# Cross-attention block: one copy carries a slot of k and q together, into rows six partitions apart

## The reference, cut to what matters

```python
x = layer_norm(hidden_states, ln1_w, ln1_b)
q = (x @ q_w + q_b).reshape(B, LQ, H, HD).transpose(0, 2, 1, 3)
k = (encoder_hidden_states @ k_w + k_b).reshape(B, LK, H, HD).transpose(0, 2, 1, 3)
v = (encoder_hidden_states @ v_w + v_b).reshape(B, LK, H, HD).transpose(0, 2, 1, 3)
scores = jnp.einsum('bhqd,bhkd->bhqk', q, k) * scale
scores = jnp.where(mask, scores, mask_value)
attn = jax.nn.softmax(scores, axis=-1)
out = jnp.einsum('bhqk,bhkd->bhqd', attn, v)
out = out.transpose(0, 2, 1, 3).reshape(B, LQ, D)
hidden = out @ cproj_w + cproj_b + residual
y = layer_norm(hidden, ln2_w, ln2_b)
y = jax.nn.gelu(y @ fc_w + fc_b, approximate=True)
return hidden + y @ proj_w + proj_b
```

## Time and profile before

| | |
|---|---|
| median of 3 runs | 260.54 us |
| lowest and highest | 257.79 and 260.97 us |
| the profiled execution | 260.51 us |
| its span on the core | 258.7 us |
| mean granted clock of PE | 0.921 of full |

### The profile page before, as it was taken

The page is one execution under the profiler, slowest core; times in us unless marked ns, Lnnn a source line. Parts: engine busy times, 40 slices in busy tenths (PEclk is TensorE's granted clock), DMA queues, the critical chain, the costliest instruction groups (busy, mean ns, idle before and its releaser), DMA issues.

```text
span 258.7 us, 7970 instructions
## 1 busy us (share of the span) xinstructions
PE 216.3 (84%) x3324; PEld 200.9 (78%) x3324; DVE 173.4 (67%) x377; ACT 123.8 (48%) x269; POOL 86.9 (34%) x100
## 2 busy tenths in 40 slices
PE   0974089759979999999699995999999988699795
PEld 0974069649968988989599895989998987599695
DVE  2683046495799768977687593767896669349661
ACT  3568203128922785378305960278338813541050
POOL 5345121113842085128410751128414511212300
PEclk9998559776999999999979996799999999779999
DMA  6999992006900395049801892059406930100011
GB/s 204 292 208 225 186 160 90 4 8 114 125 7 4 109 179 86 5 136 141 98 3 50 172 127 27 5 159 151 62 4 121 130 44 3 44 0 3 3 41 41
DMA packets 24255, 23.10 MB, mean 89 GB/s; under 512 B 2908, under 2 KB 23964, under 8 KB 24220
## 3 DMA queue, kind: packets, MB, share of 16 engines
q1 hardware_dynamic: 21616, 19.75, 43.7%
q10 hardware_dynamic: 2604, 2.85, 4.5%
HBM read 7.62 MB, written 2.10 MB: 38 GB/s over the span
## 4 chain that ended last, share of the span: by engine, by line
PE 41%; DVE 19%; DMA 15%; SPq 13%; issue 8%; ACT 3%; POOL 1%; ACTq 0%; POOLq 0%; DVEq 0%
PE bank L1049 11%; SPq L341 10%; PE bank L1051 8%; PE bank L1050 8%; DMA k_stack<-part_k 8%; DMA k_stack<-mask_rows 5%; PE bank L1123 4%; DVE mx L813 4%; DVE recip L859 3%; PE scores L1079 3%; DVE g_hi L876 2%; PE bank L1194 2%; DMA col<-in_cols 2%; DVE st L831 1%; PE bank L1066 1%
## 5 line engine op out<-in xcount | busy, mean ns | idle before, releaser
L859 DVE RECIPROCAL recip<-bank 128x256 f32<-128x256 f32 x16 | 28.1, 1754 | 21.3 <-PE bank L1123 21.3
L1049 PE MATMUL bank<-proj_hi,g_hi 128*128 128x256 f32 x128 | 39.0, 304 | 3.7 <-DVE g_lo L878 3.6
L1049 PE MATMUL bank<-z_hi,fc_hi 128*128 128x256 f32 x128 | 38.8, 303 | 2.2 <-DVE z_lo L924 2.2
L1051 PE MATMUL bank<-proj_lo,g_hi 128*128 128x256 f32 x128 | 36.8, 287 | 0.0
L1050 PE MATMUL bank<-proj_hi,g_lo 128*128 128x256 f32 x128 | 36.8, 287 | 0.0
L1051 PE MATMUL bank<-z_lo,fc_hi 128*128 128x256 f32 x128 | 36.4, 284 | 0.0
L1050 PE MATMUL bank<-z_hi,fc_lo 128*128 128x256 f32 x128 | 36.3, 284 | 0.0
L813 DVE TENSOR_REDUCE mx<-scores 128x16 f32<-128x1024 f32 x16 | 19.5, 1221 | 24.4 <-PE scores L1079 24.4
L563 POOL TENSOR_TENSOR o_lo<-o,o_hi 128x256 fp32r<-128x256 f32 x16 | 18.3, 1142 | 46.4 <-ACT o_hi L611 46.4
L549 POOL TENSOR_TENSOR rs<-ve,power 128x1 f32<-128x1 f32 x16 | 9.8, 614 | 62.3 <-DVE ve L839 62.3
L618 ACT ACTIVATE fc_raw<-bank,fc_bias 128x256 f32<-128x256 f32 x64 | 26.5, 468 | 6.4 <-PE bank L1051 6.2
(11 more groups left out here) (121 smaller groups left out, 586.0 us busy)
## 6 DMA issues: line engine op xcount, KB each, us to landing
k_stack<-part_k SPq DMA_DIRECT2D x48, 128.0 KB, 5.0
q_stack<-part_q SPq DMA_DIRECT2D x48, 128.0 KB, 5.8
x_in<-in_x SPq DMA_DIRECT2D x8, 256.0 KB, 3.4
ctx_in<-in_ctx_t SPq DMA_DIRECT2D x7, 256.0 KB, 4.3
out<-y SPq DMA_DIRECT2D x7, 256.0 KB, 2.2
fc_raw<-in_fc_w ACTq DMA_DIRECT2D x1, 1024.0 KB, 10.4
proj_raw<-in_proj_w ACTq DMA_DIRECT2D x1, 1024.0 KB, 15.8
ctx_in<-in_ctx_t ACTq DMA_DIRECT2D x1, 256.0 KB, 4.0
```

Of the source, the lines that this page charges most:

```text
L859: ve.reciprocal(recip[:], bank7[:, 1, :, :]).then_inc(recip_made, 1)
L1049: mm(out_ap, a_hi, b_hi, start=first, stop=False, skip_group_check=True)
L1051: return mm(out_ap, a_hi, b_lo, start=False, stop=last, skip_group_check=True)
```

## The change

A slot's k and q parts travel in one copy. The six part tiles become one tile `parts` with k's three and q's three parts side by side, so that one source pattern takes part `K_SLOTS[n]` of k and part `Q_SLOTS[n]` of q. The two stacks become one tile `stack_kq`, [128, 8, 2, TT, KC, 128]: k and q lie side by side in a partition. One DMA reads [128 partitions, 2, 512] and writes 16 rows of 16 runs of 1 KB (16 KB contiguous in each row). The rows of slot n are now n, n + 6, ..., n + 90 (row of feature d: n + 6d). Six copies of 256 KB a group take the place of twelve, each waits for the later of its two parts in both names, and one semaphore counts them with the mask.

The free order inside parts and stacks is by tile first (t, m, w), so the mask row and the ones get rows of 512 elements, `turn_maxima` makes two transposes of 16 columns instead of one of 32, and ACT casts and copies 16 x 256 values instead of 32 x 128.

```diff
-LOADS_Q = len(Q_SLOTS)
-LOADS_K = len(K_SLOTS) + 1
+SLOTS = len(Q_SLOTS)
+LOADS = SLOTS + 1
-def head_pos(h):
-    return (h % 8) * 2 + h // 8
...
-        part = {(n, k): [sb(f"part_{n}{k}{s}", [P, KC, GT], BF16) for s in range(2)]
+        parts = [sb(f"parts{s}", [P, 2 * PARTS, TT, KC, P], BF16) for s in range(2)]
+        part = {(n, k): [parts[s][:, PARTS * "kq".index(n) + k, :, :, :] for s in range(2)]
-        rest = {n: sb(f"rest_{n}", [P, KC, GT]) for n in "qk"}
-        q_stack = [sb(f"q_stack{s}", [P, H, GT], BF16) for s in range(2)]
-        k_stack = [sb(f"k_stack{s}", [P, H, GT], BF16) for s in range(2)]
+        rest = {n: sb(f"rest_{n}", [P, TT, KC, P]) for n in "qk"}
+        stack_kq = [sb(f"stack_kq{s}", [P, H // KC, 2, TT, KC, P], BF16) for s in range(2)]
+        k_stack = [stack_kq[s][:, :, 0, :, :, :] for s in range(2)]
+        q_stack = [stack_kq[s][:, :, 1, :, :, :] for s in range(2)]
-        n_parts = [sb(f"n_parts{p}", [P, N_PARTS, H], BF16) for p in range(TT)]
-        n_t = [sb(f"n_t{p}", [N_PARTS * H, P], BF16) for p in range(TT)]
+        n_parts = [sb(f"n_parts{p}", [P, KC, N_PARTS, H // KC], BF16) for p in range(TT)]
+        n_t = [sb(f"n_t{p}", [N_PARTS * H // KC, KC * P], BF16) for p in range(TT)]
...
         def _(sp):
-            def stack_part(g, k, name, slots, stacks, stacked, made):
-                sp.wait_ge(made[k], g.count(1, 1))
-                for n in range(len(slots)):
-                    if slots[n] == k:
-                        sp.dma_start(stacks[g.slot][HD * n:HD * (n + 1), :, :]
-                                     .rearrange("r (h m) t -> r h (m t)", m=KC),
-                                     part[name, k][g.slot][:].rearrange("p m t -> p (m t)")) \
-                          .then_inc(stacked[g.slot], 16)
             def stack_mask(g):
-                sp.dma_start(k_stack[g.slot][MASK_ROW:MASK_ROW + 1, :, :],
-                             mask_rows[g.c:g.c + 1, :].unsqueeze(1).broadcast_to([1, H, GT])) \
-                  .then_inc(k_stacked[g.slot], 16)
-            def stack_k(g, parts=range(PARTS)):
-                for k in parts:
-                    stack_part(g, k, "k", K_SLOTS, k_stack, k_stacked, (k_lead, k_second, k_third))
-            def stack_q(g, parts=range(PARTS)):
-                for k in parts:
-                    stack_part(g, k, "q", Q_SLOTS, q_stack, q_stacked, (q_lead, q_second, q_third))
+                sp.dma_start(k_stack[g.slot][MASK_ROW:MASK_ROW + 1].rearrange("r h t m w -> r h (t m w)"),
+                             mask_rows[g.c:g.c + 1].rearrange("r t m w -> r (t m w)").unsqueeze(1)
+                             .broadcast_to([1, H // KC, KC * GT])) \
+                  .then_inc(stacked[g.slot], 16)
+            def stack_parts(g):
+                for k in range(PARTS):
+                    sp.wait_ge((k_lead, k_second, k_third)[k], g.count(1, 1))
+                    sp.wait_ge((q_lead, q_second, q_third)[k], g.count(1, 1))
+                    for n in range(SLOTS):
+                        if max(K_SLOTS[n], Q_SLOTS[n]) == k:
+                            k_at, q_at = K_SLOTS[n], PARTS + Q_SLOTS[n]
+                            sp.dma_start(stack_kq[g.slot][n:MASK_ROW:SLOTS]
+                                         .rearrange("r h s t m w -> r (h s) (t m w)"),
+                                         parts[g.slot][:, k_at:q_at + 1:q_at - k_at]
+                                         .rearrange("p s t m w -> p s (t m w)")) \
+                              .then_inc(stacked[g.slot], 16)
                 load_ctx(Group(0, 2))
-                stack_k(a, (0,))
-                stack_q(a, (0,))
-                for k in (1, 2):
-                    stack_k(a, (k,))
-                    stack_q(a, (k,))
-                sp.wait_ge(stacks_set[0], 32)
+                stack_parts(a)
+                sp.wait_ge(stacks_set[0], 16)
                 sp.wait_ge(mask_ready, 1)
             def second_step(a, b):
-                sp.wait_ge(stacks_set[1], 32)
+                sp.wait_ge(stacks_set[1], 16)
                 stack_mask(a)
-                stack_k(a, (0,))
-                stack_q(a, (0,))
-                for k in (1, 2):
-                    stack_k(a, (k,))
-                    stack_q(a, (k,))
+                stack_parts(a)
                 load_row(pb_rows, proj_b)
...
-            def lead(g, n, made, bank, bias, stacked, per_load, first):
+            def lead(g, n, made, bank, bias, first):
                 act.wait_ge(made, g.count(1, 1))
-                wait(act, stacked[g.slot], g.loads(per_load, before=1))
+                wait(act, stacked[g.slot], g.loads(16 * LOADS, before=1))
                 for m in range(KC):
-                    last = sc.activation(part[n, 0][g.slot][:, m, :], bank[:, m, :], ACT.Identity, bias=bias[:, m:m + 1])
+                    last = sc.activation(part[n, 0][g.slot][:, :, m, :], in_tiles(bank[:, m, :]), ACT.Identity,
+                                         bias=bias[:, m:m + 1])
                 last.then_inc(first, 1)
...
-                act.dma_start(q_stack[g.slot][SCORE_ROWS:SHIFT_ROWS, :, P * p:P * p + P], n_t[p][:]) \
+                act.dma_start(q_stack[g.slot][SCORE_ROWS:SHIFT_ROWS, :, p, :, :]
+                              .rearrange("r h m w -> r h (m w)"), n_t[p][:]) \
...
-            def set_stack(s, stacks):
-                act.dma_start(stacks[s][MASK_ROW:SHIFT_ROWS, :, :],
-                              one_rows[:].unsqueeze(1).broadcast_to([SHIFT_ROWS - MASK_ROW, H, GT])) \
+            def set_stack(s):
+                act.dma_start(stack_kq[s][MASK_ROW:SHIFT_ROWS].rearrange("r h s t m w -> r (h s) (t m w)"),
+                              one_rows[:].unsqueeze(1).broadcast_to([SHIFT_ROWS - MASK_ROW, H, KC * GT])) \
...
-                lead, rest = [n_parts[p][:, k, :].rearrange("p (i w) -> p w i", w=2) for k in range(N_PARTS)]
+                lead, rest = [n_parts[p][:, :, k, :] for k in range(N_PARTS)]
...
-                    last = ve.scalar_tensor_tensor(rest[n][:, m, :], bank[:, m, :], bias[:, m:m + 1],
-                                                   part[n, 0][g.slot][:, m, :], ALU.add, ALU.subtract)
+                    last = ve.scalar_tensor_tensor(rest[n][:, :, m, :], in_tiles(bank[:, m, :]), bias[:, m:m + 1],
+                                                   part[n, 0][g.slot][:, :, m, :], ALU.add, ALU.subtract)
...
-                        rows = slice(S * (2 * p + b), S * (2 * p + b) + S)
+                        rows = slice(S * b, S * b + S)
-                                  q[0:SCORE_ROWS, head_pos(h), rows], k[0:SCORE_ROWS, head_pos(h), rows],
+                                  q[0:SCORE_ROWS, h % 8, p, h // 8, rows], k[0:SCORE_ROWS, h % 8, p, h // 8, rows],
...
                     pe.wait_ge(n_kept, g.count(2, 1))
-                mm(n_t_ps, n_parts[p][:].rearrange("p k h -> p (k h)"), ident_b[:], start=True, stop=True,
-                   skip_group_check=True).then_inc(n_turned, 1)
+                for m in range(KC):
+                    last = mm(n_t_ps[:, P * m:P * m + P], n_parts[p][:, m, :, :].rearrange("p k h -> p (k h)"), ident_b[:],
+                              start=(m == 0), stop=True, skip_group_check=True)
+                last.then_inc(n_turned, 1)
...
-                            rows = slice(S * (2 * p + b), S * (2 * p + b) + S)
+                            rows = slice(S * b, S * b + S)
-                                pos = head_pos(2 * (4 * s + i) + par)
+                                h = 2 * (4 * s + i) + par
-                                          k[0:SHIFT_ROWS, pos, rows], q[0:SHIFT_ROWS, pos, rows],
+                                          k[0:SHIFT_ROWS, h % 8, p, h // 8, rows],
+                                          q[0:SHIFT_ROWS, h % 8, p, h // 8, rows],
...
-                pe.wait_ge(k_stacked[g.slot], g.loads(16 * LOADS_K))
-                pe.wait_ge(q_stacked[g.slot], g.loads(16 * LOADS_Q))
+                pe.wait_ge(stacked[g.slot], g.loads(16 * LOADS))
```

More of the change, by code:

```diff
@@ L149, in build @@
         mask_u8 = sb("mask_u8", [G, GT], U8)
-        mask_rows = sb("mask_rows", [G, GT], BF16)
-        one_rows = sb("one_rows", [SHIFT_ROWS - MASK_ROW, GT], BF16)
+        mask_rows = sb("mask_rows", [G, TT, KC, P], BF16)
+        one_rows = sb("one_rows", [SHIFT_ROWS - MASK_ROW, KC * GT], BF16)
         x_in = [sb(f"x_in{s}", [P, TT, D]) for s in range(3)]
@@ L207, in build @@
         bank7 = psum("bank7", [P, 2, KC, P])
-        n_t_ps = bank4[0:N_PARTS * H, 0, 0:P]
+        n_t_ps = bank4[0:N_PARTS * H // KC, 0, 0:KC * P]
         w_loaded = {n: sem(f"w_loaded_{n}") for n in ("q", "k", "v", "c", "fc", "proj")}
@@ L217, in build @@
         ctx_loaded = [sem(f"ctx_loaded{s}") for s in range(2)]
-        q_stacked = [sem(f"q_stacked{s}") for s in range(2)]
-        k_stacked = [sem(f"k_stacked{s}") for s in range(2)]
+        stacked = [sem(f"stacked{s}") for s in range(2)]
```

(24 more changed lines are left out.)

## The result

| | before | after |
|---|---|---|
| median | 260.71 us (257.79 to 260.97) | 247.86 us (246.16 to 248.90) |
| profiled execution | 260.51 us | 246.96 us |
| its span | 258.7 us | 245.2 us |
| its mean granted clock of PE | 0.921 | 0.944 |

The ratio is 0.9525 with a 95% interval of 0.9432 to 0.9618: faster. The forecast was 248.1 us.

What follows compares the result with a forecast made beforehand. PE, busy 84% of the span, was taken as the bound, idling for stack and mask copies. 260.51 - 8.5 (steps) - 5.5 (beginning) + 1.6 (second matmul) = 248.1 us, range 243.5 to 257.

Steps and rivals of the forecast that it cites:

- part 1: Stack copies: six of 256 KB replace twelve, each writing across 91 partitions; a KB falls from 145 to 88 ns.
- the choice of 88 ns: Engine time per KB of stack copy, taken as the geometric middle of the bounds 53 and 145 ns.
- the 71 to 104 of the forecast: Range of ns per KB of stack copy in the main case: 246.5 to 250 us, chance 0.50.
- part 3: Full steps: copies land before PE asks, so stalls before scores go; 7.5 us plus 0.97 in the last, together 8.5.
- part 4: The beginning: faster stack copies let the mask land sooner, first scores at 28.0 us; gain 5.5 us, bounds 0 and 8.9.
- From 14.5 us on the DMA engines are never free: In the beginning, the premise that DMA engines stay busy, behind the gain of 5.5 us.
- 97 x (145 - 88): In the beginning, 96 stack packets and the mask's on the last engine, times ns saved: 5.5 us.
- this load holds the stacks back: Sign of being wrong: first scores unmoved while steps gain, if the load of proj_raw holds the mask copy back.
- part 5: turn_maxima as two matmuls: a second costs 0.10 us (bounds 0.05 to 0.23), 1.6 us for sixteen; ScalarE's larger cast hidden.
- The packet time stays: Rival, chance 0.12: 145 ns is the price of SBUF to SBUF copies, not of the destination; 262 us, the same within 2%.
- The spread makes packets slower: Rival, chance 0.05: engines walking rows in distant partitions collide more; slower by 2% from 151 ns, 276 us at 170 ns.
- As good as loads: Rival, chance 0.16: stack copies at 53 to 70 ns, beginning gains 7.3 to 8.9 us; 245 to 246 us.

Runs made afterwards that it cites:

- spread_only: The kernel before with one edit: each of its twelve 128 KB copies writes rows six apart instead of 16 neighbouring ones; 247.74 us, ratio 0.9415.
- merge_only: The changed kernel with each slot back in 16 neighbouring rows, still six joined copies of 256 KB; 288.52 us, ratio 1.0819.
- proj_later: The changed kernel with ScalarE issuing the load of proj_raw at 23.70 instead of 17.29 us; 248.36 us, ratio 0.9458.
- merge_turns: The changed kernel with slots in 16 neighbouring rows, and slots 3, 4 and 5 in rows 64, 80 and 48 onward; 283.40 us, ratio 1.0856.
- step_three: The changed kernel with three slots interleaved in 48 rows, so a slot's rows stand three apart; 250.05 us, ratio 0.9618.
- step_two: The changed kernel with two slots interleaved in 32 rows, so a slot's rows stand two apart; 249.77 us, ratio 0.9478.
- warm: The changed kernel with 54 matmuls of no use added on PE before the first scores; 248.05 us, ratio 0.9546.
- warm_both: The changed kernel with 54 useless matmuls before the first scores and 10 and 14 more where PE waits in second_step; 248.06 us, ratio 0.9538.

## Why the prediction was right

**What the copies cost (part 1 and the choice of 88 ns).** Right in kind; in size 79 ns in the beginning, near the 88, and 62 in a full step, under the 71 to 104 of the forecast. The reading behind it, that where a copy writes is what makes it slow, is shown by spread_only, one edit that gives the whole gain (61 ns for a KB in a step instead of 145), and from the other side by merge_only (180 ns). What the neighbouring rows crowd was not shown.

**Steps (part 3).** The stall is gone, as forecast. The gain was 10.1 us, not 8.5. It was right to price it by step lengths and not by waits: two waits of 2.52 and 2.6 us went, and their steps came down by 3.41 and 4.99 us. Behind the first wait the granted clock was 0.60 from 130 to 132 us, and 0.50 from 160 to 162 us in the next step; how much of the difference it makes was not measured. The term was mis-sized because the two steps of 25.1 us that served as the measure were not clean: they went to 24.79 and 24.64. The first still had a wait of 0.27 us before its scores. The other follows the longest stall, and 0.48 of its 0.54 us lie ahead of its first `shift`, 1.30 us after the store instead of 0.82, and not at its own copies. The step with a stall of 0.97 us went from 25.02 to 24.13.

**The beginning (part 4).** Mis-sized: 3.6 us instead of 5.5, and for two reasons. The step that failed is "From 14.5 us on the DMA engines are never free". This was read in the kernel before, and the change itself undid it, since slot 0 waits for q's lead and the next three for the seconds: 2.0 us of idle engines. The other is the 145 in 97 x (145 - 88), which is the price in a step. In the beginning it was 97 ns, as the earlier trace rows with its 95 could have told, and it went to 79: 97 x 18 = 1.7 us, an estimate from the two rows. With 2.0 us of idle engines against it this term alone gives nothing. The 3.6 us measured must owe something to the load of `proj_raw`, which shares the engines and landed 6.4 us after its issue instead of 15.8, but no run separates that. That this load holds the stacks back, named as a way to be wrong, is true too (3.6 us of the first scores in proj_later). So the 5.5 came near for a reason that was only in part the right one.

**The second matmul (part 5).** Priced at 1.6 us, it is nearly free. In the full steps of after the two together take 0.28 us (L1077), against 0.23 for the one, so a second costs 0.05 us there, the lower of the two bounds. The steps of after and spread_only, which keeps the single one, differ by 122.92 - 122.68 = 0.24 us over five steps with ten pairs, so about 0.4 us for sixteen, an estimate from one profile each that puts the whole difference down to it. ScalarE's cast went from 0.25 to 0.36 us and was hidden as said.

So the forecast took off 8.5 + 5.5 - 1.6 = 12.4 us, and the profiled executions differ by 13.5, made of 10.1 + 3.6 - 0.3 + 0.1 (the second matmul lies inside the 10.1). That 248.1 and 247.86 are so near owes something to errors that cancelled: too little for the steps, too much for the beginning and for the matmul.

**Rivals.** "The packet time stays" was priced at 262 us with joined copies at 145 ns. No run had that: in packed rows the joined copies took 180 ns (merge_only) and 1.16 x 6 x 16 / 691 KB = 161 (merge_turns, 133 to 139 us), and the kernels 288.5 and 283.4 us. What the prediction had not seen is that joining itself makes packed copies slower. Even its sum for slower packets, 260.5 + 1.6 + 6 x 0.096 x (180 - 145), gives only 282, since it leaves out that in the beginning and in all steps the bytes now start later. "The spread makes packets slower" fell: they became faster. "As good as loads" was nearest for the rate in a step (62 ns), but not for the time, as its gain in the beginning did not come.

## What to carry to other kernels

In this kernel a copy from SBUF to SBUF is faster when its 16 destination rows are not neighbours (in a step 61 ns for a KB in spread_only, 145 in before). Laying them out with a step cost the matmul that contracts over them nothing (a score matmul has a median of 196 ns in before and after), and this one edit of the destination slice was worth 5 to 6%. Joining copies saves issue time (six of 0.61 us a group in after, twelve of 0.60 in before), but each joined copy waits for the later of its sources: with spread rows twelve copies did as well as six, and with the load of 1 MB moved out of the way they did better (243.55 against 248.36 us). An undisturbed step of a stalling kernel is not a clean measure of the step without stalls: its own wait may only just be covered, and it may begin with what the step before left over. And a price per KB that is read in one stage need not hold in another, here 145 ns in a step and 97 in the beginning for the same copies.

## What the runs showed of the hardware

- The rate of copies between partitions depends on how the 16 destination rows stand: 109 to 120 GB/s for neighbouring rows in copies of 256 KB (merge_only, merge_turns), 127 to 132 in copies of 128 KB in the stalling steps and 197 in the beginning (before), 202, 213 and 233 for three, two and six apart (step_three, step_two, after). The DMA share is 1.1 to 1.2 in these stretches, at 109 GB/s (merge_only, 1.19) as at 233 (after, 1.13), so a full share says nothing of the rate.
- PE's clock did not stay up for 54 added matmuls (warm): held at 1.00 to 29 us, it was 0.61 on average from 32 to 35, with PE at work throughout that stretch after 1.77 us of waiting. In warm_both it held to 38 us and was 0.50 from 41 to 44, again with PE at work throughout.
- A higher granted clock need not shorten anything: warm_both's profile has 0.965 over its span and after's 0.944, at 247.82 and 246.96 us.
